# A gated recurrent block on one Trainium2 core: the rotation regrouped by head pair, and the gate's projection put behind the score products of y

## The reference, cut to what matters

```
proj = xn @ in_proj_w.T            # z, x, B, C, dt, theta, lambda
Bm = rms(B) * w + B_bias           # one B and C per token, biased for each head
Cm = rms(C) * w + C_bias
tc = cumsum(theta)                 # 32 angles per head
rope(v) = [v1*cos(tc) - v2*sin(tc), v1*sin(tc) + v2*cos(tc)]
Bm, Cm = rope(Bm), rope(Cm)
h  = alpha*h + gamma*x(B) + beta*previous x(B)      # per head, over 1024 tokens
y  = (h C + D x) * silu(z)
s  = rms(y) * norm_w @ out_proj_w.T
out = u + s * silu(fp8(xn) @ fp8(ffn_w).T + ffn_b)
```

## Time and profile before

| what | value |
|---|---|
| median of 3 runs | 1400.39 us |
| profiled execution | 1400.26 us |
| its span | 1398.5 us |
| PE busy | 1143.9 us (82%) |
| DVE busy | 1270.9 us (91%) |
| ACT busy | 779.7 us (56%) |
| POOL busy | 747.2 us (53%) |
| granted TensorE clock, mean of the run | 0.929 |

### The profile page before, as it was taken

The page is one execution under the profiler, slowest core; times in us unless marked ns, Lnnn a source line. Parts: engine busy times, 40 slices in busy tenths (PEclk is TensorE's granted clock), DMA queues, the critical chain, the costliest instruction groups (busy, mean ns, idle before and its releaser), DMA issues. The chain is left out here.

```text
span 1398.5 us, 30923 instructions
## 1 busy us (share of the span) xinstructions
PE 1143.9 (82%) x11508; PEld 840.5 (60%) x11508; DVE 1270.9 (91%) x1998; ACT 779.7 (56%) x1184; POOL 747.2 (53%) x563
## 2 busy tenths in 40 slices
PE   3466269998999999999999899999998999899810
PEld 2355146666666666666667666766676666667610
DVE  5887479998999899999999999989998999899778
ACT  2222136665666666666666666666666666666431
POOL 3410035665666656655666566656665666566523
PEclk9665579999999999999999999999999999999965
DMA  7121324222422242224222423233333322222123
GB/s 171 39 83 60 94 61 108 63 63 66 108 63 63 65 108 63 63 65 108 62 63 66 96 70 67 65 80 77 66 69 73 75 63 65 62 63 63 32 87 94
DMA packets 66673, 103.83 MB, mean 74 GB/s; under 512 B 14003, under 2 KB 30876, under 8 KB 66204
## 3 DMA queue, kind: packets, MB, share of 16 engines
q1 hardware_dynamic: 66524, 101.85, 31.1%
HBM read 24.73 MB, written 9.96 MB: 25 GB/s over the span
## 5 line engine op out<-in xcount | busy, mean ns | idle before, releaser
L1168 POOL TENSOR_TENSOR rot<-part 128x512 f32<-128x512 f32 x256 | 382.5, 1494 | 540.7 <-DVE part L1005 489.0
L1005 DVE SCALAR_TENSOR_TENSOR part<-bcs,k_prmT,trig 128x512 f32<-128x512 f32 x512 | 501.1, 1029 | 0.9 <-DMA trig<-tri 0.9
L1117 ACT ACTIVATE E<-d 128x512 f32<-128x512 f32 x256 | 151.7, 592 | 184.2 <-PE d L825 181.9
L843 PE MATMUL s<-rot 64*128 64x128 f32 x2048 | 149.7, 285 | 23.7 <-POOL rot L1168 19.2
L1023 DVE TENSOR_TENSOR M<-s,E 128x512 f32<-128x512 f32 x256 | 163.5, 678 | 2.4 <-PE s L843 1.8
L843 PEld LDWEIGHTS s<-rot 64*128 64x128 f32 x2048 | 126.9, 188 | 62.1 <-issue 54.7
L1177 POOL TENSOR_TENSOR ce<-rot,eb 128x512 f32<-128x512 f32 x128 | 160.0, 1271 | 3.0 <-ACT eb L1139 3.0
L1199 POOL TENSOR_TENSOR sqa<-sqa,sq 128x512 f32<-128x512 f32 x112 | 142.6, 1273 | 14.2 <-ACT sq L1122 6.2
L935 PE MATMUL y<-M,xk 128*64 128x128 f32 x2048 | 140.1, 279 | 0.0
L857 PEld LDWEIGHTS o<-k_w_o,yT 128*128 128x128 f32 x1024 | 132.5, 191 | 10.4 <-DVE yT L1082 5.0
L857 PE MATMUL o<-k_w_o,yT 128*128 128x128 f32 x1024 | 134.5, 275 | 2.6 <-DVE yT L1082 2.6
(11 more groups left out here) (242 smaller groups left out, 1827.8 us busy)
## 6 DMA issues: line engine op xcount, KB each, us to landing
trig<-tri SPq DMA_DIRECT2D x512, 128.0 KB, 2.4
bcs<-bc_t SPq DMA_DIRECT2D x16, 256.0 KB, 4.1
bcs<-bc_t SPq DMA_DIRECT2D x32, 128.0 KB, 4.1
a_big<-in_L_attn_u SPq DMA_DIRECT2D x4, 512.0 KB, 6.2
xn_t<-a_xnT SPq DMA_DIRECT2D x1, 2048.0 KB, 7.6
tc_t<-a_tcT SPq DMA_DIRECT2D x1, 2048.0 KB, 12.4
bc_t<-a_tmp SPq DMA_DIRECT2D x1, 2048.0 KB, 7.4
tcs<-tc_t SPq DMA_DIRECT2D x8, 256.0 KB, 3.0
```

What stands on the lines that cost most here:

```text
L843: last = nc.tensor.matmul(Sp[j][:, k], rot[rows, q % 2, p, 0, k], rot[rows, q % 2, p, 1, k], start=True, stop=True)
L1005: nc.vector.scalar_tensor_tensor(out=part[:, 2 * p + f, :], in0=bcs[:, (t + q // NQ) % 2, 2 * w + f, :], scalar=col, in1=trig[:, p, 1 - f, ...
L1117: nc.scalar.activation(E[:, h % 2, :], Dp[:], ACT.Exp).then_inc(e_ready, 1)
L1168: nc.gpsimd.tensor_tensor(rot[:, q % 2, p, w, :], part[:, 2 * p, :], part[:, 2 * p + 1, :], ALU.add).then_inc(rot_ready, 1)
```

## The change

It does three things. The rotation's eight products are regrouped by head pair: four of pair 0 (B, then C) ahead of `ang`, and four of pair 1 behind xk and xc. `part` has two buffers for B and two for C, where it had two for each pair. Each sum now waits for all four products of its pair, and POOL does two sums ahead of ce and two behind it. M of h = 2 and 3 now stands ahead of xk and xc, right behind the states. On PE the gate's projection moves behind the products of y, and the transposes of B for pair 1 move behind the first exponents and scores. The counts in the waits (for the sums and for the copies) follow the new order. No instruction is added or removed.

```diff
@@ spread (SP)
-                    sp.wait_ge(part_ready, at(T8, t, 8 * (q - 1) + 6 + 2 * p))
+                    sp.wait_ge(part_ready, at(T8, t, 8 * (q - 1) + 4 + 4 * p))
@@ scores (PE)
-                pe.wait_ge(rot_ready, at(T4, t, 4 * q + 3 + p))
+                pe.wait_ge(rot_ready, at(T4, t, 4 * q + 2 * p + 2))
@@ the unit's loop on PE
                     if q > 0:
                         project(t, q - 1, (2, 3))
                     for p in range(2):
-
-                        if live(t, q + 1):
-                            pe.wait_ge(xk_ready, at(T2, t, 2 * q + 2 + p + 1))
-                        w = K["w_zx"][:, (2 * q + p) * P:(2 * q + p + 1) * P]
-                        nc.tensor.matmul(R[p][:], w, xns[:, t % 2, :], start=True, stop=True).then_inc(z_ready, 1)
-
-                    for p in range(2):
                         pe.wait_ge(m_ready, at(T4, t, 4 * q + 2 * p + 2))
...
+                    for p in range(2):
+
+                        if live(t, q + 1):
+                            pe.wait_ge(xk_ready, at(T2, t, 2 * q + 2 + p + 1))
+                        w = K["w_zx"][:, (2 * q + p) * P:(2 * q + p + 1) * P]
+                        nc.tensor.matmul(R[p][:], w, xns[:, t % 2, :], start=True, stop=True).then_inc(z_ready, 1)
+
                     pe.wait_ge(ce_ready, at(T2, t, 2 * q + 2))
...
-                    for p in range(2):
-                        pe.wait_ge(rot_ready, at(T4, t, 4 * (q + 1) + p + 1))
+                    def b_next(p):
+                        pe.wait_ge(rot_ready, at(T4, t, 4 * (q + 1) + 2 * p + 1))
                         pe.wait_ge(sz_ready, at(T2, t, 2 * q + p + 1))
                         b_by_token(q + 1, p)
+
+                    b_next(0)
...
                     exponents(t, q + 1, 0)
                     scores(t, q + 1, 0)
+                    b_next(1)
                     exponents(t, q + 1, 1)
@@ the unit's loop on DVE
                     if live(t, q + 1):
-                        rotation(t, q + 1, 0, 0, 0)
+                        rotations(t, q + 1, 0)
                     if live(t, q + 2):
                         angles(t, q + 2)
                     for c in range(CS):
                         state(t, q, c)
-                    if live(t, q + 1):
-                        rotation(t, q + 1, 0, 0, 1)
-                        x_scaled(t, q + 1, tn, 0)
-                        x_scaled(t, q + 1, tn, 1)
                     scores(t, q, 2)
                     scores(t, q, 3)
                     if live(t, q + 1):
-                        for p, w in ((1, 0), (0, 1), (1, 1)):
-                            rotation(t, q + 1, p, w, 0)
-                            rotation(t, q + 1, p, w, 1)
+                        x_scaled(t, q + 1, tn, 0)
+                        x_scaled(t, q + 1, tn, 1)
+                        rotations(t, q + 1, 1)
@@ sums and the unit's loop on POOL
-                pool.wait_ge(part_ready, at(T8, t, 8 * q + 2 * k + 2))
+                pool.wait_ge(part_ready, at(T8, t, 8 * q + 4 * p + 4))
...
                     if live(t, q + 1):
-                        sums(t, q + 1, 0)
+                        for k in range(2):
+                            sums(t, q + 1, k)
                     c_decayed(t, q)
                     if live(t, q + 1):
-                        for k in range(1, 4):
+                        for k in range(2, 4):
                             sums(t, q + 1, k)
```

More of the change, by code:

```diff
@@ L997, in rotation @@
                 col = K["prmT"][:, 16 * (1 + 2 * w + f) + pair:16 * (1 + 2 * w + f) + pair + 1]
-                k = 2 * w + p
                 if w == 0 and f == 0:
@@ L1003, in rotation, with rotations @@
                 if f == 0:
-                    dve.wait_ge(rot_ready, at(T4, t, 4 * q + k - 1))
-                nc.vector.scalar_tensor_tensor(out=part[:, 2 * p + f, :], in0=bcs[:, (t + q // NQ) % 2, 2 * w + f, :], scalar=col,
+                    dve.wait_ge(rot_ready, at(T4, t, 4 * q + 2 * p + w - 1))
+                nc.vector.scalar_tensor_tensor(out=part[:, 2 * w + f, :], in0=bcs[:, (t + q // NQ) % 2, 2 * w + f, :], scalar=col,
                                                in1=trig[:, p, 1 - f, :], op0=ALU.add, op1=ALU.mult).then_inc(part_ready, 1)
+            def rotations(t, q, p):
+                for w in range(2):
+                    for f in range(2):
+                        rotation(t, q, p, w, f)
             def b_decayed(t, q, tt):
@@ L1028, in _ @@
             x_scaled(0, 0, 0, 1)
[L1029 to L1032, removed]
+            rotations(0, 0, 0)
+            rotations(0, 0, 1)
             b_decayed(0, 0, 0)
@@ L1163, in sums @@
             def sums(t, q, k):
-                w, p = k // 2, k % 2
-                pool.wait_ge(part_ready, at(T8, t, 8 * q + 2 * k + 2))
+                p, w = k // 2, k % 2
+                pool.wait_ge(part_ready, at(T8, t, 8 * q + 4 * p + 4))
                 pool.wait_ge(y_ready, at(T2, t, 2 * q - 2))
-                nc.gpsimd.tensor_tensor(rot[:, q % 2, p, w, :], part[:, 2 * p, :], part[:, 2 * p + 1, :],
+                nc.gpsimd.tensor_tensor(rot[:, q % 2, p, w, :], part[:, 2 * w, :], part[:, 2 * w + 1, :],
                                         ALU.add).then_inc(rot_ready, 1)
```

## The result

| | before | changed |
|---|---|---|
| median | 1399.28 us (4 runs) | 1667.16 us (4 runs, 1660.36 to 1677.99) |
| ratio | | 1.1931, 95% interval 1.1879 to 1.1983 |
| profiled execution | 1400.26 us | 1677.99 us |
| granted clock, mean of the run | 0.929 | 0.874 |

A forecast was written before the change was run, and what follows sets the result against it. DVE, 95% busy, was taken to bound the kernel, with 3.4 us of slack in the ring of waits. Adding 3.16, 1.98 and 1.2 us made 20.36 us a unit; with block ends and first units +161 us: 1561 us, range 1505 to 1610.

The forecast's parts named there:

- the ring: Waits from x on PE through ACT and DVE to the next unit's x: 14.0 us before, 20.36 after.
- the five links: Parts of a unit: x to y 4.00, to first E 9.14, to M's end 2.33, to ang 4.17, to x 0.72 us.
- Step 2: On DVE, four products stand ahead of ang in place of one: +1.98 us a unit.
- step 3: On DVE, pair 0's four products wait for its copies and POOL's second sqa before they get through: +1.2 us a unit.
- Step 1: On PE, y's products for both pairs now stand ahead of z: +3.16 us a unit, and y starts no earlier.
- all the slack: In the kernel before, the waits needed 14.0 us of a 17.4 us unit, leaving 3.4 us.
- slow copies: Rival: the fourth copy's landing grows up to 4.4 us, a unit is 21.5 us, the whole 1627 us; chance 6%.
- PE from x to the start of z: 4.00 us: First stretch on PE, read from the kernel before as 593.78 - 589.78 and kept at 4.00 us for the changed one.
- the third rival: TensorE's clock falls: PE at half speed from x to y, 4 us more a unit, 1810 us; chance 5%.

The follow-up runs named there:

- experiment 5: The changed kernel with pair 0's four products moved behind ang and the states, the gate's projection still behind y: 1422.68 us, ratio 1.0181.
- the filled kernel: The changed kernel with ten extra products of no use on PE where it waits for ang, in the units q > 0: 1586.87 us, ratio 1.1353.
- experiments 4 and 7: Each the changed kernel with one edit: 4 puts the gate's projection back ahead of y, 1520.83 us; 7 puts the sines ahead of the silu, 1524.10 us.
- experiment 5 with the sines early: The changed kernel with pair 0's products behind ang and the states, and ACT's sines ahead of the silu: 1349.10 us, 0.9648 of the kernel before.

## Why the prediction was wrong in size and right in kind

- *What bounds the kernel before:* right. The kernel before with the sines early, at 1.0005, shows that the ring was not the bound; that DVE was is read from its rows, and the earlier trace rows.
- *The ring and its length:* right. With the clock held inside the blocks, a unit took 20.81 us against 20.33 forecast, and the whole 1587 us against 1561. Four of the five links agree one by one. Step 2 (products ahead of ang) with step 3 is confirmed by experiment 5, which takes them off the ring.
- *Step 1, that the gate's move buys nothing and costs 3.16 us:* the cost is right as a link (y to the first E, 9.26 against 9.14). As a sole change it used up all the slack and cost 1.8 us a unit on top (19.58 against 17.79 over all 62 steps).
- *Step 3, copies and sqa:* 4.25 us against 4.17 from M to ang in the mean, but that is in part luck, since two kinds of units are mixed in it. In 39 of the 62 units the fourth copy lands 2.4 to 2.6 us after its issue, as in the earlier trace rows, and DVE waits 0.5 to 0.9 us for it. In 23 it lands 3.5 to 4.5 us after it, and DVE waits 1.7 to 2.7 us. So the rival "slow copies", given 6%, was true of more than a third of the units. In the filled kernel a unit inside a block takes 20.69 us in the mean against 20.36, which is 16 us over 48 units, and a block end 23.1 us in place of 21.5, which is 11 us; together they are about the 26 us by which it is above the forecast. The clock has a share in the block ends.
- **The term that failed** is the first of the ring, "PE from x to the start of z: 4.00 us", taken over unchanged from a kernel whose PE waited less than 1 us each time in the units, but for one wait of 1.5. It measured 5.77 (x to y in the changed kernel, where z has left this stretch). The cause was on the list as the third rival, "TensorE's clock falls", with 5% and 4.0 us a unit. I weighed the unit's mean load (78%, "nearer to 92 than to 40") and called the waits short, when a single wait ahead of x was enough. Its price was about 1.7 us a unit. The filling shows 80 us, 1667 to 1587. My 4 us assumed half speed for the whole work of the stretch; in 31 of the 54 units the clock came back within it, and only in 16 did the low clock last for most of it.
- *The rivals:* the two stacked. The forecast's range was built from cases that excluded each other, but a ring that makes PE wait 2.3 us is just what brings the clock down. The two should have been added: x to y took 5.85 us in the mean of the 54 units q > 0, and 1561 + 54 x 1.85 = 1661.

The Trainium skill, "TensorE: Matmul & The Clock Gate", section "Why this matters for your kernels", warns against idle gaps between bursts. The traces agree in kind: with waits of 2.0 to 4.0 us ahead of x, 47 of 54 units were slow in the changed kernel, 12 of 54 with the wait half filled, and none with it filled. In size they go further than the page, whose row names longer gaps than most of these: in experiments 4 and 7 waits of 1.76 to 2.34 us were enough in 84 of 108 units. Waits of 1.25 to 1.7 us elsewhere in the unit did no harm that shows. The prediction named the page and gave the rival 5%, while the trace before had no such gap to tell; no evidence is not evidence against.

## What to carry to other kernels

A reorder that removes no work can only pay on the engine that sets the time, and it can lengthen the ring of waits that the steps of one iteration close; so walk once round the ring in the profile and count its slack before moving anything on it, the ACT work and the DMA issues included. If the ring becomes the bound, TensorE will wait once an iteration: price that wait as wait plus clock. Work that needs no late input (here the sines) belongs ahead of the instruction that waits for one.

## What the runs showed of the hardware

- Ten extra products of 0.23 us placed into a wait made a kernel 80 us (5%) faster. The stretch behind the wait shrank from 5.8 to 4.1 us, and that is the clock's.
- Sines right behind the silu need no table load; a silu right behind the sines needs one. In the kernel before there are two loads of 1.28 us a unit; with the sines first there are three, as these rows of ACT in experiment 5 with the sines early show. It still pays, since ACT waited there.

```profile
574.40 1.28 ACT L1111 ACT_TABLE_LOAD   x1
...
577.48 1.28 ACT L1147 ACT_TABLE_LOAD   x1
579.15 0.60 ACT L1147 ACTIVATE sz<-r 128x512 f32<-128x512 f32 x1 [0.39 <-PE r L936]
...
580.63 1.28 ACT L1119 ACT_TABLE_LOAD   x1
```

- A 128 KB copy inside SBUF costs SP 0.64 us of its queue, so a row of eight takes 5 us and more; the fourth of them sets when pair 0's products can start. Now and then one takes 1.1 to 2.1 us instead (16 of 512 in the kernel before, 19 in the changed one). In the changed kernel it is nearly always the sixth of the eight, and then the fourth copy, issued before it, lands 3.5 to 4.2 us after its issue instead of 2.4. In the unit at 814.26 us the sixth issue took 2.06 us, the fourth copy landed after 4.23, and DVE waited 2.45 us for it. Why stays open.
